# Position weights with the batch vectors stationary, and rows moved inside SBUF

## The reference, cut to what matters

```python
def _L1_xattn_ref(x, layer_idx, weight):
    w = weight[layer_idx]
    return jnp.einsum('bsd,sod->bso', x, w)

x = x + _L1_xattn_ref(_layernorm(x, axis=-1), itok_S_0_31, ctx_1024)
```

## Time and profile before

| | |
|---|---|
| median of three runs | 1635.64 us |
| profiled execution, its own time | 1635.95 us |
| its span | 1634.2 us |
| busy PE, PEld | 1352.3 us (83%), 858.0 us (53%) |
| busy DVE, ACT, POOL | 1028.2 us (63%), 895.0 us (55%), 611.5 us (37%) |
| span of the stage's products on TensorE | 1280.5 to 1335.2 us |
| last addition to X in this stage | ends at 1344.8 us |

### The profile page before, as it was taken

How to read it: one execution, slowest core, us unless ns; L and a number is a source line. 1 busy time by engine, 2 the same in 40 slices (tenths; PEclk the granted TensorE clock), 3 DMA queues, 4 the chain that set the end, 5 groups by cost and what they waited for, 6 DMA issues and landing times. The chain is left out here.

```text
span 1634.2 us, 42235 instructions
## 1 busy us (share of the span) xinstructions
PE 1352.3 (83%) x12665; PEld 858.0 (53%) x12727; DVE 1028.2 (63%) x3858; ACT 895.0 (55%) x1709; POOL 611.5 (37%) x901
## 2 busy tenths in 40 slices
PE   2399999995999999976664999999995786989998
PEld 0155555553565655645532666666663773545554
DVE  2277777773566666645433788888877335766774
ACT  1177777773677777753323677777773232223221
POOL 3467777751222222211000576667661211211120
PEclk9999999997899999998985999999997557999999
DMA  5000000000000000000003576676774000000000
GB/s 149 1 2 2 0 0 0 1 2 1 1 2 0 0 0 0 0 2 1 0 0 91 157 195 186 187 203 182 188 198 117 1 0 1 7 8 13 6 7 13
DMA packets 147221, 78.58 MB, mean 48 GB/s; under 512 B 6673, under 2 KB 146066, under 8 KB 147010
## 3 DMA queue, kind: packets, MB, share of 16 engines
q1 hardware_dynamic: 146610, 75.45, 17.0%
q0 software_dynamic: 528, 2.10, 0.4%
HBM read 41.62 MB, written 35.91 MB: 47 GB/s over the span
## 5 line engine op out<-in xcount | busy, mean ns | idle before, releaser
L715 POOL TENSOR_TENSOR rr<-ms_eps,minus_half 128x16 f32<-128x16 f32 x64 | 184.7, 2903 | 92.2 <-DVE ms_eps L926 92.2
L469 PE MATMUL psum<-identb,stacks 128*128 128x128 bf16 x1800 | 144.8, 226 | 31.7 <-DVE stacks L462 21.6
L1047 DVE TENSOR_REDUCE rowmax<-psum 128x4 f32<-128x768 f32 x128 | 122.1, 954 | 71.4 <-PE psum L1946 71.1
L1210 DVE CUSTOM_DVE_ANT_0 summed<-psum,pos_score 128x128 f32<-128x128 f32 x512 | 118.0, 286 | 57.8 <-PE psum L2143 46.9
L469 PEld LDWEIGHTS psum<-identb,stacks 128*128 128x128 bf16 x1800 | 112.7, 101 | 65.0 <-DVE stacks L462 31.4
L965 DVE TENSOR_REDUCE rowmax<-psum 128x4 f32<-128x512 f32 x128 | 88.2, 689 | 58.0 <-PE psum L1822 56.8
L476 ACT ACTIVATE qT<-psum 128x1024 bf16<-128x1024 bf16 x96 | 99.5, 1036 | 30.0 <-PE psum L469 30.0
L1767 ACT ACTIVATE pos_rows<-psum 128x512 f32<-128x512 f32 x72 | 43.0, 597 | 128.8 <-PE psum L2283 123.0
L560 PE MATMUL psum<-probsT,values 128*32 128x128 f32 x2048 | 109.3, 285 | 2.0 <-DVE attn L586 1.2
L1638 ACT ACTIVATE pos_rows<-psum 128x512 f32<-128x512 f32 x128 | 76.5, 597 | 60.9 <-PE psum L2135 58.4
L768 POOL TENSOR_TENSOR rest<-staged,stacks 128x128 f32<-128x128 f32 x32 | 13.7, 428 | 231.0 <-ACT stacks L452 231.0
(11 more groups left out here) (243 smaller groups left out, 3358.0 us busy)
## 6 DMA issues: line engine op xcount, KB each, us to landing
skew<-pos_rows SPq DMA_DIRECT2D x128, 258.0 KB, 4.4
pos_score<-skew SPq DMA_DIRECT2D x128, 256.0 KB, 4.1
X<-in_x_dram POOLq DMA_DIRECT2D x1, 2048.0 KB, 12.0
ctxT<-in_ctx_dram SPq DMA_DIRECT2D x1, 2048.0 KB, 10.5
out_dram<-X SPq DMA_DIRECT2D x8, 256.0 KB, 2.3
w_up<-in_L_ffn_w_e_dram SPq DMA_DIRECT2D x2, 512.0 KB, 4.2
w_down<-in_L_ffn_w_e_dram SPq DMA_DIRECT2D x2, 256.0 KB, 6.0
consts<-in_consts_dram SPq DMA_DIRECT2D x1, 401.0 KB, 3.3
```

What stands on the lines that cost most here:

```text
L469: last = pe.transpose(turned[:, t, :], stacks[:, which, 2 * t:2 * t + 2, :].rearrange("s h k -> s (h k)"), identb[:, :])
L715: pool.tensor_tensor(out=rr[:, par, i * H:(i + 1) * H], in0=ms_eps[:, i * H:(i + 1) * H], in1=minus_half[:, 0:H], op=ALU.pow).then_inc(A.r ...
L1047: dve.tensor_reduce(rowmax[:, par, first:first + 2 * PT - 1:2].rearrange("s (b h) -> s b h", b=2), B.max_space, AX.X, ALU.max, negate=True ...
L1210: last = dve.tensor_tensor_reduce(summed[:, r % 2, p, :], P.score_bank[r % 2][:, p, :], pos_score[:, par, r * PT + p, :], 1.0, -3.0e38, AL ...
```

## The change

The operands of the product change places. The stationary operand is now the 32 batch vectors of a position (32 columns), the moving one the 128x128 matrix (128 columns). The result of a position, 32 batch rows by 128 outputs, goes to a quarter of the partitions (a = j % 4) and a quarter of the bank's columns (c = j // 4). `save_y` copies the bank as it stands into y_chunk[k] (the memory of `hidden`), once the transfers of the chunk two before have landed (E.moved[k]). SP then moves each position's 32x128 block into its one partition of yT, with yT now [s, b, o]: 16 transfers a chunk, 128 in all. Steps `stage` and `turn_back` go; DVE waits for all 128 transfers and adds eight groups from yT. TensorE's loop over the pairs is written out.

```diff
--- before.py
+++ after.py
@@ -209,7 +209,7 @@
         itok = sb("itok", [1, S], I32)
         gathered = pos_score[:, :, :, :]
         yT = sb("yT", [D, NB, S])
-        y_stage = hidden[:, :, :, :]
+        y_chunk = hidden[:, :, :, :]
 
 
         projected = yT[:, 0:16, :].rearrange("s (a w) (h d) -> s a w h d", a=4, h=H)
@@ -324,11 +324,11 @@
         P.shared_v, P.stacked = None, True
         P.attn_space, P.y_space = P.ln_bank[:, 128:128 + S], P.ln_bank[:, 256:256 + D]
         E = Phase()
-        [E.by_pool, E.by_dve, E.by_act, E.mm, E.ev, E.st, E.turned, E.x] = sems(
-            "e", "by_pool by_dve by_act mm ev st turned x")
+        [E.by_pool, E.by_dve, E.by_act, E.mm, E.ev, E.x] = sems("e", "by_pool by_dve by_act mm ev x")
+        E.moved = sems("e_moved", "0 1")
         share_norm(E, 3 * NB + NB // 4)
         E.ln_bank = bank[5]
-        E.y_bank, E.turn_bank = bank[0:2], bank[2:4]
+        E.y_bank = bank[0:2]
 
         def ln_group_stats(dve, q, g, par):
 
@@ -680,6 +680,14 @@
                 sp.dma_start(w_down[p * FW:(p + 1) * FW, 0:TILES - 1, :], pairs[p]).then_inc(ld.f, 16)
             sp.dma_start(w_down[:, TILES - 1, :], t["L1_ffn_w2_s"]).then_inc(ld.f, 16)
             sp.dma_start(spread[:, :, :], t["spread"].rearrange("k (t m) -> k t m", t=TILES - 1)).then_inc(ld.f, 16)
+            sp.wait_ge(F.cast, 1)
+            for chunk in range(8):
+                k = chunk % 2
+                sp.wait_ge(E.ev, chunk + 1)
+                for c in range(4):
+                    for a in range(4):
+                        sp.dma_start(yT[16 * chunk + 4 * c + a:16 * chunk + 4 * c + a + 1, :, :],
+                                     y_chunk[a * NB:(a + 1) * NB, k, c, :]).then_inc(E.moved[k], 16)
             for g in range(NG):
                 sp.wait_ge(F.x, g + 1)
                 sp.dma_start(out[4 * g:4 * g + 4].rearrange("b s d -> s b d"), X[:, 4 * g:4 * g + 4, :]).then_inc(done.out, 16)
@@ -1294,10 +1302,10 @@
                     gather(pair, 1)
 
                 def residual_group(g, par):
-                    wait(dve, E.turned, g + 1)
-                    dve.tensor_tensor(X[:, at(4 * g, 4), :], X[:, at(4 * g, 4), :],
-                                      E.turn_bank[par].rearrange("s (b d) -> s b d", b=4), ALU.add).then_inc(E.x, 1)
-
+                    dve.tensor_tensor(X[:, at(4 * g, 4), :], X[:, at(4 * g, 4), :], yT[:, at(4 * g, 4), :], ALU.add).then_inc(E.x, 1)
+
+                dve.wait_ge(E.moved[0], 4 * 256)
+                dve.wait_ge(E.moved[1], 4 * 256)
                 with dve.Fori(0, NB // 8) as pair:
                     residual_group(2 * pair, 0)
                     residual_group(2 * pair + 1, 1)
@@ -1719,28 +1727,20 @@
 
                 def save_y(pair, k):
                     wait(act, E.mm, 2 * pair + k + 1)
-                    act.activation(yT[:, :, at(32 * pair + 16 * k, 16)],
-                                   E.y_bank[k].rearrange("o (s b) -> o b s", b=NB), ACT.Copy).then_inc(E.ev, 1)
+                    wait(act, E.moved[k], 256 * pair)
+                    act.activation(y_chunk[:, k, :, :].rearrange("b c o -> b (c o)"), E.y_bank[k], ACT.Copy).then_inc(E.ev, 1)
 
                 gather(0, 0)
                 gather(0, 1)
-                with act.Fori(0, 3) as pair:
+                for k in range(2):
+                    save_y(0, k)
+                    gather(1, k)
+                with act.Fori(1, 3) as pair:
                     for k in range(2):
                         save_y(pair, k)
                         gather(pair + 1, k)
                 save_y(3, 0)
                 save_y(3, 1)
-
-                def stage(g, par):
-                    wait(act, E.turned, g - 1)
-                    act.activation(y_stage[:, par, :, :], yT[:, at(4 * g, 4), :], ACT.Copy).then_inc(E.st, 1)
-
-                act.wait_ge(E.ev, 8)
-                stage(0, 0)
-                stage(1, 1)
-                with act.Fori(1, NB // 8) as pair:
-                    stage(2 * pair, 0)
-                    stage(2 * pair + 1, 1)
 
             position_weights()
 
@@ -2235,28 +2235,15 @@
                     wait(pe, E.by_act, GATHER_ACT[1] * (2 * pair + k + 1))
                     wait(pe, E.ev, 2 * pair + k - 1)
                     for j in range(16):
-                        last = pe.matmul(E.y_bank[k][:, j * NB:(j + 1) * NB].unsqueeze(2), gathered[:, k, j, :],
-                                         seqT[:, :, at(32 * pair + 16 * k + j)], start=True, stop=True)
+                        a, c = j % 4, j // 4
+                        last = pe.matmul(E.y_bank[k][a * NB:(a + 1) * NB, c * D:(c + 1) * D], seqT[:, :, at(32 * pair + 16 * k + j)],
+                                         gathered[:, k, j, :], start=True, stop=True)
                     last.then_inc(E.mm, 1)
 
-                def turn_back(g, par):
-                    wait(pe, E.st, g + 1)
-                    wait(pe, E.x, g - 1)
-                    for k in range(4):
-                        last = pe.transpose(E.turn_bank[par][:, k * S:(k + 1) * S], y_stage[:, par, k, :], ident)
-                    last.then_inc(E.turned, 1)
-
                 pe.wait_ge(E.xnT, E.base + NB // 4)
-                multiply(0, 0)
-                multiply(0, 1)
-                with pe.Fori(1, 4) as pair:
+                for pair in range(4):
                     multiply(pair, 0)
                     multiply(pair, 1)
-                turn_back(0, 0)
-                turn_back(1, 1)
-                with pe.Fori(1, NB // 8) as pair:
-                    turn_back(2 * pair, 0)
-                    turn_back(2 * pair + 1, 1)
 
             position_weights()
```

## The result

The changed kernel takes 1666.79 us in the median of its runs (1664.29 to 1676.79), the kernel before, beside it, 1637.37 us (1635.48 to 1645.11). The ratio is 1.018, with a 95% interval of 1.013 to 1.022: slower by 29 us. Forecast were 1662 us and a slower kernel.

A forecast was written before the change was run, and what follows sets the result against it. SP's issues were taken to bound the changed stage: first issue 1284.3, 127 x 0.62 us, landing 2.3 and additions 5.6 end it at 1370.9, +26.2 us on 1635.95. Forecast 1662 us, its own range 1652 to 1679, 8 in 10 1643 to 1688.

The forecast's parts named there:

- Products: TensorE's 128 products with swapped operands: 2.9 us a chunk at clock 0.50 in place of 6.8, no longer the bound.
- Gathers: POOL's six copies a chunk, which stay: 4.8 us a chunk, less than SP's 9.9 us.
- The issue: SP's queue of 128 transfers: 0.62 us each start to start, 9.9 us a chunk, the new bound of the stage.
- Landing and additions: Stage's end: last block lands 2.3 us after its issue, then DVE's eight additions take 5.6 us, none hidden.
- The sum: Stage's last addition ends at 1370.9 us against 1344.77, +26 us; the experts' 290 us only move.
- Cheap issues: Rival: SP's issues cost 0.40 to 0.47 us, below 0.54, so the kernel is not slower, 1634 to 1643 us; chance 0.19.
- The target partition as the bound: Rival: 32 pieces land nearly one after another in one partition, up to 0.99 us a transfer, +74 us, 1710; chance 0.14.
- The estimate of 0.60 us for each target partition: By the skill's port rule one partition takes 16 KB in 0.60 us, 128 transfers 77 us however fast SP issues; sum 1660.
- The gathers as the bound: Rival: issues under 0.3 us, chunks 4.8 us apart, last save at 1318, end near 1326, -18 us, 1617; chance 0.02.

The follow-up runs named there:

- turned on TensorE: Changed kernel without the transfers: four transposes a chunk on TensorE restore the old layout, then the old way back runs; 1617.77 us, ratio 0.986.
- four apart: Changed kernel with 32 transfers of 64 KB, each to four target partitions that lie 4 partitions from each other; 1618.72 us, ratio 0.986.
- half-byte kernel: Changed kernel with 128 transfers of 8 KB in place of 16 KB, only batches 16 to 31 moved; 1672.24 us, ratio 1.019.
- four positions a transfer: Changed kernel with 32 transfers of 64 KB, each into four neighbouring (near) target partitions; 1623.22 us, ratio 0.989.
- two queues: Changed kernel with the same 128 transfers, half of them issued by ACT behind its gathers for the next chunk; 1655.26 us, ratio 1.009.
- the 256 KB that go to DRAM in one transfer: Changed kernel with each chunk sent out through DRAM and brought back in four transfers of 64 KB, 40 in all; 1626.86 us, ratio 0.992.

## Why the prediction was right

**Products.** It said that they leave the bound whatever they cost, and so it was. The size was off: 2.9 us a chunk was taken, from doubling; 2.0 was measured at clock 0.50 (and 1.25 at 1.00, where 1.44 was taken). All that this could move is SP's start, and that is 3.80 us after the first product, as predicted (1284.3 - 1280.5): ACT's tenth copy ends late enough to hide the rest.

**Gathers.** 4.8 us a chunk. In the changed kernel they are hidden under SP. With the transfers gone from the bound, chunks came by 4.6 us (turned on TensorE) and, from the third save on, 4.5 to 5.1 us (four apart).

**The issue.** This term decided, as it was said to. 0.62 us was taken, from the 64-partition loads and w_down; 0.642 was measured, 127 x 0.022 = 2.8 us more. The half-byte kernel and the one with four positions a transfer show that it is a price per transfer, and the one with two queues that it is paid on the queue. The choice of the row was the important step: itok has one partition as well and costs 0.40, and from it the kernel would have come out no slower. The choice went by likeness, and two of the rows behind it (w_qr and w_kr 0.47 and 0.91) are lengths of an issue, not times from start to start; that 0.62 came so near is in part luck. Which property of the added transfer makes it dear stays open, and the guess that differently cut sides do was borne out in size only. The runs narrow it: neither the bytes nor 16, 32 or 128 source partitions changed much (0.64, 0.64 and 0.59 us start to start), while the 256 KB that go to DRAM in one transfer have an issue of 0.34 us in the median.

**Landing and additions.** 2.3 and 5.6 us taken; 2.2 us of landing measured, 2.6 from the start of the last issue to the first addition, and eight additions in 4.9 us, 0.61 each. That is 0.7 us less for the additions. They were priced by two additions in a row that read a bank of PSUM; now both operands are in SBUF, which may be the reason and wasn't tried alone.

**The sum.** +26.2 predicted for the stage, +28.7 measured: +2.8 for the issues, -0.7 for the additions, the rest is a few tenths. The experts' 289.4 us are the same, as said.

**The rivals.** Cheap issues: refuted by 0.642 us. The target partition as the bound: refuted by half the bytes. The estimate of 0.60 us for each target partition had given 1660, nearly the forecast's 1662, so the time alone could not have told the two apart. Its 77 us count all 128 transfers one behind another whoever issues them, and that is not borne out: with near targets the same 2 MB took 39 us from the first issue (1288.6) to the last landing (1327.9). The gathers as the bound: wrong for this kernel, and what happens once the count of transfers falls to 32. Its time for that case was 1617; the kernel with targets four apart took 1618.72. That nearness is luck: the last save comes at 34.7 us in place of 37.5 (1318 - 1280.5), and the way from there to the last landing takes 5.4 us in place of 2.3: 1.8 for the last chunk's issues, which the sum left out, and 3.6 for the landing.

The medians differ by 29 us and the profiled executions by 41 (1676.79 against 1635.95). Some 12 us of that arose in unchanged code ahead of the stage. Why executions differ there stays open.

## What to carry to other kernels

A transfer has a price on the queue that issues it, here 0.64 us, and 128 small ones are 82 us of a queue however few bytes they hold; where a change replaces compute by many small transfers, count the issues first, and choose the layout so that one transfer reads from all partitions: 32 of those were no dearer each than 128 small ones. Where a stage has no busy engine and no busy DMA, look at the queues, which are not counted as busy. And take the change apart before giving it up: the products in this one gained some 20 us (1617.77 against 1638.41 us of the kernel before, run beside it) once their results came back by transposes on TensorE (32 more than before the change) or by 32 transfers.

## What the runs showed of the hardware that was not expected

- The clock did not scale a burst in full. The same 16 products took 2.00 us at a granted clock of 0.50 and 1.25 us at 1.00, four transposes 1.12 and 0.66 us (both in the kernel that turns on TensorE): factors of 1.6 and 1.7, not 2. Ends of matmuls are modelled in the trace, so part of this may be the model's.
- The length of an issue on SP hardly depends on how much one of these transfers carries: 0.55 us in the median for 128 source partitions and 64 KB, 0.59 for 32 source partitions and 16 KB and for 16 and 8 KB. It does depend on the transfer's form: itok and w_gate have 0.36 us each.
- Landing times of 16-KB transfers inside SBUF were flat, 2.1 to 2.7 us over 128 of them at 26 GB/s; from two queues whose blocks of issues started together the last ones took up to 9.5 us, at a DMA share of 1.04 for 32 GB/s, where 53 GB/s had needed 0.23 a few us before.
